# Graph layer with mixer and experts: the edge list prepared in pieces between the windows of the first transformation, the first layer's root product made in its own loop, empty tiles skipped

## What is computed

```python
def _rgcn_layer(x, W, root, bias, src, dst, seg):
    agg = jax.ops.segment_sum(x[src], seg, num_segments=N_REL * N_NODES)
    agg = agg.reshape(N_REL, N_NODES, -1)
    return jnp.einsum('rnd,rde->ne', agg, W) + x @ root + bias
...
xn = _layernorm(x, axis=-1)
x = x + _L0_gnn_ref(xn, ..., edge_index, edge_type_8) + _L0_mix_ref(xn[None], ...)[0]
x = x + _L0_ffn_ref(_layernorm(x, axis=-1)[None], ...)[0]
```

## Time and profile before

| what | us |
|---|---|
| median of 3 runs | 6951.84 |
| lowest and highest | 6949.16, 6957.95 |
| profiled execution: its own time | 6953.12 |
| profiled execution: its span | 6951.0 |
| PE, POOL, DVE, ACT busy in the span | 5505.9, 4779.5, 2098.9, 1056.1 |
| granted TensorE clock, mean | 0.921 of full speed |

### The profile page before, as it was taken

One profiled execution on the slowest core, in us unless ns is written; L12 is line 12 of the kernel. 1 busy time (PEld: TensorE's weight loads), 2 busy tenths in 40 slices (PEclk: granted clock), 3 DMA queues, 4 the chain that ended last, 5 costly groups with the idle time before them and its releaser, 6 DMA issues.

```text
span 6951.0 us, 83677 instructions
## 1 busy us (share of the span) xinstructions
PE 5505.9 (79%) x22959; PEld 4023.7 (58%) x22959; DVE 2098.9 (30%) x5751; ACT 1056.1 (15%) x2704; POOL 4779.5 (69%) x4994
## 2 busy tenths in 40 slices
PE   4886777777777777888888888886788888888888
PEld 2344555555555554666666666664677677776676
DVE  2332211221212212233232332232344444444443
ACT  1221111111111110111111111111122222222222
POOL 0113777777777776777777777775777777777775
PEclk9998888998898988999999999998999999999998
DMA  4444444444444444444544445445333333333333
GB/s 119 138 138 136 135 139 142 136 136 145 136 136 135 140 141 122 142 142 143 147 144 142 141 143 150 142 142 141 110 115 113 112 112 115 114 113 112 113 114 76
DMA packets 358935, 906.06 MB, mean 130 GB/s; under 512 B 96549, under 2 KB 183309, under 8 KB 339819
## 3 DMA queue, kind: packets, MB, share of 16 engines
q0 software_dynamic: 233856, 638.89, 31.8%
q10 hardware_dynamic: 116050, 257.82, 12.7%
q1 hardware_dynamic: 8662, 4.79, 0.3%
HBM read 709.15 MB, written 192.01 MB: 130 GB/s over the span
## 4 chain that ended last, share of the span: by engine, by line
POOL 43%; issue 23%; PE 23%; DMA 8%; DVE 2%; POOLq 1%; DVEq 0%; ACT 0%; ACTq 0%; SPq 0%
POOL ring L433 43%; PE ps_out L1218 10%; DMA ring<-table,gather_idx 8%; PE ps_y L1193 4%; PE ps_y L1429 2%; PE ps_tr L1361 2%; PE ps_c L1349 1%; DVE onehot L860 1%; PE ps_c L1440 1%; PE ps_b L1440 1%; PE ps_b L1349 1%; PE ps_c L1319 0%; POOLq L428 0%; DVE r L1095 0%; PE ps_a L1387 0%
## 5 line engine op out<-in xcount | busy, mean ns | idle before, releaser
L433 POOL DMA_INDIRECT ring<-table,gather_idx x4872 | 4721.4, 969 | 1579.8 <-issue 1533.2
L1218 PE MATMUL ps_out<-ring,onehot 128*125 x7200 | 1987.6, 426 | 941.3 <-DVE onehot L860 919.9
L1218 PEld LDWEIGHTS ps_out<-ring,onehot 128*125 128x125 f32 x7200 | 1439.1, 209 | 1364.5 <-issue 1146.6
L860 DVE TENSOR_TENSOR onehot<-targets,nodes_now 128x500 f32<-128x500 f32 x900 | 604.1, 680 | 1881.5 <-SPq L372 1710.8
L1218 PE MATMUL ps_out<-ring,onehot_more 128*125 x3720 | 954.6, 401 | 265.8 <-DVE onehot_more L860 228.8
L1193 PE MATMUL ps_y<-W,hT 128*125 128x512 f32 (+1 forms) x2400 | 1067.4, 586 | 11.0 <-issue 9.3
L1218 PEld LDWEIGHTS ps_out<-ring,onehot_more 128*125 128x125 f32 x3720 | 688.5, 194 | 497.2 <-issue 406.7
L1193 PEld LDWEIGHTS ps_y<-W,hT 128*125 128x125 f32 x2400 | 471.3, 202 | 449.2 <-issue 416.8
L860 DVE TENSOR_TENSOR onehot_more<-targets,nodes_now 128x250 f32<-128x250 f32 x930 | 372.9, 421 | 931.9 <-PE ps_out L1218 528.1
L449 ACT COPY y_stage<-ps_y 125x512 f32<-125x512 f32 x350 | 205.2, 586 | 2356.6 <-PE ps_y L1193 2355.2
L1429 PE MATMUL ps_y<-hT,big 128*128 128x125 f32 x3200 | 428.8, 284 | 0.0
(11 more groups left out here) (186 smaller groups left out, 3141.3 us busy)
## 6 DMA issues: line engine op xcount, KB each, us to landing
table<-y_stage ACTq DMA_DIRECT2D x150, 1008.0 KB
ring<-table,gather_idx POOLq DMA_INDIRECT x4872
base_in<-table ACTq DMA_DIRECT2D x150, 125.0 KB
table<-y_stage ACTq DMA_DIRECT2D x150, 117.0 KB
x_in<-in_x_dram ACTq DMA_DIRECT2D x100, 125.0 KB
xn_in<-xn_scratch ACTq DMA_DIRECT2D x100, 125.0 KB
xn_scratch<-xn_in ACTq DMA_DIRECT2D x50, 125.0 KB
res_scratch<-res_win ACTq DMA_DIRECT2D x50, 125.0 KB
```

The costliest lines, as they stand in the source:

```text
L433: nc.gpsimd.indirect_dma_start(ring[:, c * D:(c + 1) * D], None, table[l], bass.IndirectOffsetOnAxis(ap=gather_idx[:, tile:tile + 1].bitca ...
L860: return nc.vector.tensor_tensor(out, targets[:, bass.ds(col, count)].unsqueeze(2).broadcast_to([128, count, n]), nodes.unsqueeze(1).broad ...
L1218: return nc.tensor.matmul(ps_out[w % 2][0:WIN, 0:D], lhsT, ring[:, bass.ds(slot + j * D, D)], start=first, stop=last)
```

## The change

- **The prelude is dissolved.** The steps of the edge list are cut into pieces (`prepare`): row numbers in window 8 of phase 0, the other reductions in windows 9 to 12, one pair of transposes in each of the windows 10 to 22 (`ROWS_AT`, `TB` = 13), the window bounds in windows 23 to 27. PE makes a pair of transposes after the products of that window, into `ps_out`, and DVE copies it out in the same window. The parameter loads other than the weights are issued by SP behind the edge list.
- **Phase 0.** The nodes are loaded four windows ahead (`x_bufs`: `x_in` and `base_in`). The statistics of a window are made one window early, so POOL's power lies beside other work; the mixer's power is made once for all windows (125x50). PE waits for each bank by itself, not for all of the window before, and the root block is no longer made.
- **The root product of layer 1** is made in phase 1 from two more transposes of `xn_in` (`xnT`, copied by ACT) and summed into `ps_out`. DVE adds the bias from SBUF, and `base_in` isn't loaded in this loop.
- **The table** has 8 rows for a node, gathers take row `src * 8 + type`. In phases 1 and 2 the root rows go to a tensor of their own (`base_dram`) with a third store for each window.
- **Empty tiles.** POOL doesn't gather the last three chunks of a layer, which hold no edge, and SP passes them on without a wait. DVE and PE still take them, with one-hot matrices that are zero.

```diff
+    LAST_CHUNKS = -(-edges // (TILE * TILES)) - (BODIES - 1) * RING
...
-    table = [nc.dram_tensor(f"table{l}", [nodes * ROWS, D], FP32).ap() for l in range(3)]
+    table = [nc.dram_tensor(f"table{l}", [nodes * R, D], FP32).ap() for l in range(3)]
...
+    base_dram = [nc.dram_tensor(f"base{l}", [nodes, D], FP32).ap() for l in (1, 2)]
...
+        x_bufs = [*x_in, *base_in]
...
-        ORDER = (1, 0, 4, 2, 3)
+        ORDERS = [(1, 0, 2, 3)] + [(1, 0, 4, 2, 3)] * 2
...
-            with pool.Fori(0, 2 * NW) as i:
-                pool.wait_ge(var_ready, i + 1)
-                nc.gpsimd.tensor_tensor(rstd[:, :], mv[:, 1:2], neg_half[:, :], ALU.pow).then_inc(rstd_ready, 1)
...
+            nc.gpsimd.tensor_tensor(ln1_scale[:, :], ln1_mv[:, :, 1], neg_half[:, :].broadcast_to([WIN, NW]),
+                                    ALU.pow).then_inc(rstd_ready, 1)
...
+                        if chunk >= CHUNKS - RING + LAST_CHUNKS:
+                            continue
...
+                if phase:
+                    act.dma_start(rows(base_dram[phase - 1], w), y_stage[parity][:, R * D:ROWS * D]
+                                  ).then_inc(table_stored[parity], 16)
...
+            for i in range(4):
+                act.dma_start(x_bufs[i][:, :], rows(t["x"], i)).then_inc(x0_loaded[i], 16)
+                if i == 0:
+                    load_W(0)
...
                 act.dma_start(rows(xn_dram, w), xn_in[parity][:, :]).then_inc(xn_stored[parity], 16)
+                if w + 4 < NW:
+                    act.dma_start(x_bufs[w % 4][:, :], rows(t["x"], w + 4)).then_inc(x0_loaded[w % 4], 16)
...
+            def transposed_rows(b):
+
+                for i in (2 * b, 2 * b + 1):
+                    dve.wait_ge(prep_tr, i + 1)
+                    nc.vector.tensor_copy((gather_idx, targets)[i % 2][:, b * 128:(b + 1) * 128],
+                                          ps_out[i % 2][:, 0:128]).then_inc(prep_ev, 1)
...
+                if w + 1 < NW:
+                    statistics(w + 1)
+                if w >= 2:
                     dve.wait_ge(xn_stored[parity], turn * 16)
...
+                if prev:
+                    evac_y(0, prev)
...
+                nc.vector.bn_aggr(ln1_mv[:, w, :], stats[:, :]).then_inc(ln1_ready, 1)
+                prepare(w)
...
-                    if b == 1 and not first:
+                    if phase == 0 and b == 1 and w:
+                        pe.wait_ge(y_evac_dve, w)
+                    if phase == 0 and b != 1 and w:
+                        pe.wait_ge(y_evac_act, (w - 1) * 3 + (0, 2, 3).index(b) + 1)
...
                 if prev:
                     products(0, prev)
+                if ROWS_AT <= w < ROWS_AT + TB:
+                    transposed_rows(w - ROWS_AT)
...
+                pe.wait_ge(xnT_ready, w + 1)
+                for k in range(K):
+                    nc.tensor.matmul(ps_out[w % 2][0:WIN, 0:D], xnT[:, k, :], root0[:, k, :], start=False, stop=False)
```

348 lines of the change are left out of this document (197 added, 151 removed).

## The result

| kernel | median us | lowest, highest | ratio to before, 95% interval |
|---|---|---|---|
| before (4 runs beside it) | 6950.5 | 6940.2, 6958.0 | |
| changed (4 runs) | 6736.9 | 6733.0, 6745.5 | 0.9695 [0.9679, 0.9712] |

The change makes the kernel faster by 3.05%, 214 us; 6794.5 was forecast. The profiled execution of the changed kernel took 6745.45 us, its span is 6743.7 us, 207.3 less than that of before.

A forecast was written before the change was run, and what follows sets the result against it. POOL's gathers were taken to bound the layers, and latencies over one DMA queue phase 0. From 6953.1 us, 128.6 for phase 0 and 32 for layer ends came off and 2 were added: 6794.5, range 6738 to 6868.

The forecast's parts named there:

- first product: Start of phase 0: first product at 22.5 us instead of 95.5, gain 73; ends 19 and 28.
- 50 plain windows: Phase 0: a window falls from 10.2 to 7.5 us, gain 136 over 50; range 367 to 400 us.
- the prelude's transfers: Phase 0: transfers moved out of the prelude add almost fully, loss 35 us; ends 5 and 60.
- 13 pairs: Pieces in phase 0's windows: 13 pairs of transposes at 2.6 us, 34, plus 11 for clock dips, loss 45.
- power over 125x50: End of phase 0: one POOL power ahead of the gathers, cover 13 us, price 0 to 14, taken as 0.
- end of products: Phase 0: its products end at 477.5 us against 606.1, gain 128.6.
- empty tiles: Layer ends: the last chunks need no wait, gain 10, 12 and 10 us; range of the sum 24 to 37.
- third stores: End of phases 1 and 2: a third store of 125 KB costs 0.5 to 2 us, taken as 1 each.
- The queue stays the pace: Phase 0: rival in which windows take 9.3 us, gain 63.6 and 30, total 6859; chance 22%.
- Nothing in the way: Phase 0: rival in which old transfers fit idle slots and pieces bring no dip, gain 185, total 6738; chance 20%.
- The gathers slow down: Layers: rival in which the 8 KB node step costs chunks 1.4 us more each, total about 8480; chance 4%.
- Phase 1 turns to PE: Phase 1: rival in which 65 us of extra PE products come to light, total 6859; chance 5%.

The follow-up runs named there:

- the kernel with SP silent: The changed kernel, but SP issues nothing until the nodes of window 5 are normalised, and the pieces start at window 14 instead of 8: 6743.7 us, ratio 0.9685.
- the third group: The four kernels measured last on one chip, where the kernel before took 8450.5 us; ratios to it from 0.9701 to 0.9918.
- the kernel with the ends turned: The changed kernel with the tile ends turned by PE before their store and an own semaphore for the root block's store: 8235.0 us, ratio 0.9749.

## Why the prediction was right, and where its sizes were off

The sign, the places and the mechanism were right; the sizes were not: the gain was 207.7 us between the two profiled executions where 158.6 was forecast. Three terms of phase 0 were put too dear (the windows by 21 us, the transfers by 16, the pairs by 18), and the layers gave 6 less. By its own steps:

| step | forecast | measured |
|---|---|---|
| first product | 22.5 us | 22.19 |
| 50 plain windows | 375 | 354 (7.09 each) |
| the prelude's transfers | 35 | 18.8: 10.8 in windows 1 to 4, 8.0 at the tile ends |
| 13 pairs | 45 | 27.3 (2.1 each) |
| power over 125x50 | 0, cover 13 | 0; 8.33 long, 3.1 to spare |
| end of products | gain 128.6 | 182.8 (last copy 606.27, now 423.49) |
| empty tiles | gain 32 | 13.1 + 11.8 + 10.5 = 35.4 |
| third stores | 2 | 4.0, and some at the copy of `hT` |
| layers as a whole | gain 30 | 23.9 |

**The window** was mis-sized by 0.4 us, 21 in all. I added the transposes with their duration of 0.4 us, while the distance between two starts is 0.22 (303.06 to 303.28): work on one engine overlaps at its ends, so starts have to be taken, as I did for the blocks. And I set 7.5 above my own floor of 7.35 for a queue that turned out to have room: its share is 0.63, and with four windows of nodes in store no plain window from 240 to 415 us waits for a load. The rival "The queue stays the pace" (9.3 a window) lives in the kernel with two buffers, which is at 10.4. So the likeliest case was right because of the depth, and I had named the depth only as one of three reasons.

**The transfers** cost half of what I forecast. The work that moves was seen rightly, but it doesn't add fully: where the nodes are in store or the window before has slack, other transfers pass beside them. The Trainium skill's rule, "DMA: Bandwidth & Descriptors", "Issuing engines are not separate DMA queues", that transfers run on the same 16 DMA engines whichever engine issues them, holds in its direction, as the kernel with SP silent shows with 16 us gained up to window 9 and 14.0 given back behind it; the amount in the changed kernel, 18.8, lay in the lower half of my range of 5 to 60. The place at the tile ends was expected; that it would be a single table store that is late wasn't.

**The pairs** have the mechanism that I described, DVE behind PE's products, with 1.67 us of idle PE for 2 forecast and 2.1 in all for 2.6; the clock dips that I added 11 us for didn't come: with an idle 1.67 us in each window the granted clock stays at 1.00 from 142 to 224 us. It fell to 0.50 of full speed where PE stood longer, 5.38 us before 44.59 and 8.24 before 131.24; the eight matmuls behind take 5.45 and 4.80 us for 3.60, so about 3 us of what the transfers cost are the clock's.

**The layers** gave less than forecast although the empty tiles gave more. Layer 1 gained 3.65 us: 6.5 up to its last chunk, of 13.1 that the empty tiles are worth there, since the gathers were slower by 4 ns each (6.8 us in all, open whether that is the change), and 2.9 lost behind it. The third store stood on the path twice: ACT issues it for 0.93 us ahead of the copy of `hT` that PE waits for, and the first gather waits for it to land, 1.9 and 2.1 us. I had priced only the second, at half its size. Two more differences all but cancel: the last chunk runs at full clock and is 1.6 us shorter, and the 20 matmuls of the next row take 1.7 us longer.

```profile
2503.70 0.76 ACTq L525 DMA_DIRECT2D table<-y_stage  x2
2504.49 0.93 ACTq L528 DMA_DIRECT2D base<-y_stage  x1
2505.46 0.38 ACT L539 ACTIVATE hT<-ps_tr 128x250 f32<-128x250 f32 x1 [1.79 <-issue]
2505.89 9.82 PE L1275 MATMUL ps_y<-W,hT 128*125 128x512 f32 x20 [2.63 <-ACT hT L539]
```

Where the changed kernel waits 2.63 us the kernel before waited 1.68, and its same 20 matmuls took 8.13 us. The granted clock is 0.63 and 0.55 from 2505.8 to 2510 us here and 1.00 there. In the kernels without the root product and with SP from window 5 on the same wait of 2.63 or 2.64 us is followed by 8.13 us: a wait of this length brings the lower clock in some executions and not in others.

The rival "Nothing in the way" named 6738, which the median met, but by luck, for its sizes were others: a start of 19 (22.2), windows of 367 (354), transfers of 5 (18.8), pieces of 30 (27.3). "The gathers slow down" is refuted by the table of nine rows, "Phase 1 turns to PE" by the kernel without the root product.

## What to carry to other kernels

When a loop's loads queue behind its own stores, count the time from the issue of a load to its first use in windows, and buffer past that number before anything else is tuned: here all other edits of the window gave nothing with two buffers and 1.6 us a window with four. A piece that is put between blocks should be placed where its reader has slack; the same two transposes cost 2.1 us behind the products and 0.2 in front of them. Take the length of a step on a full engine from start to start, never from durations.

## What was not expected of the hardware

- Two stores of 1664 values of 4 bytes each stood behind a stretch in which the DMA engines were full with little moved (share 1.07 at 112 GB/s, from 112 to 122 us), a table store landed late and PE stood for 8.2 us; in three other kernels with the same stores no window was long, though the stretch was there.
- One power over 125x50 on POOL took 8.33 us, one over 125x1 0.66: fifty columns cost 12.6 times one.
- The chip of the third group ran the layers a fifth to a quarter slower with every kernel, also with the kernel before (8450.5 us), while phase 0 took as long as elsewhere. POOL, which never waited for more than 0.3 us for PE's release of a ring place in the changed kernel, did so there, and the data of the gathers stopped for some microseconds at a time. The waits of POOL in the kernel with the ends turned (us in total, times, longest; `remote` is a releaser that the profile has no row for), and the slices of its DMA share in tenths and GB/s from 1218 to 1243 us:

```profile
POOL ring L503 <- PE ps_out L1328: 979.2, 347, 15.5
POOL ring L503 <- remote: 586.0, 240, 6.2
...
DMA  6161516061614161614252425151420000059999
GB/s 170 39 170 39 151 59 177 33 164 46 144 66 138 72 157 53 157 53 131 79 125 85 131 79 138 72 157 53 131 79 0 0 0 0 0 197 288 288 380 315
```

  Nothing moves for about 3 us, from 1236.8 to 1239.9. POOL starts no gather between 1234.1 and 1241.4, for it waits for PE to release a place, and up to 1238.6 DVE waits for a chunk that hasn't been reported. What makes the landings late on that chip is open; it says that the layers' 1.28 us a gather is only their pace as long as chunks land within the ring's reach.
